# Layer 2 attention: reading in array quarters, rope rows of two heads in one tile, and a new order of the stages

## The reference, cut to what matters

```python
kv_c = kv @ W_kvc                                  # 64 latent numbers a key
q_c = q @ W_dq                                     # 96 numbers a query
q_nope = (q_c @ W_uq).reshape(b, lq, H, HD)        # H = 16 heads
q_rope = _rope((q_c @ W_qr).reshape(b, lq, H, R), lq)   # R = 64
k_nope = (kv_c @ W_uk).reshape(b, lk, H, HD)
v = (kv_c @ W_uv).reshape(b, lk, H, HD)
k_rope = _rope(kv_c @ W_kr, lk)
scores = (q_nope . k_nope + q_rope . k_rope) * scale
scores = where(good, scores, NEG)                  # a window of 8 keys
out = softmax(scores) @ v
x = x + out.reshape(b, lq, H * HD) @ W_o
```

## Time and profile before

| | |
|---|---|
| median of three runs | 2151.97 us |
| the profiled execution's own time | 2150.64 us |
| its span | 2148.5 us |
| busy share: TensorE, VectorE, ScalarE, GpSimd | 83%, 70%, 46%, 45% |
| Layer 2 attention, tile loop | 739.2 to 1217 us |
| mean granted clock of TensorE | 0.91 |

### The profile page before, as it was taken

The page is one execution under the profiler, slowest core; times in us unless marked ns, Lnnn a source line. Parts: engine busy times, 40 slices in busy tenths (PEclk is TensorE's granted clock), DMA queues, the critical chain, the costliest instruction groups (busy, mean ns, idle before and its releaser), DMA issues. The chain is left out here.

```text
span 2148.5 us, 42586 instructions
## 1 busy us (share of the span) xinstructions
PE 1773.9 (83%) x14235; PEld 1327.5 (62%) x14238; DVE 1510.6 (70%) x3427; ACT 980.3 (46%) x2343; POOL 956.9 (45%) x1091
## 2 busy tenths in 40 slices
PE   6989845399797599889898789889888986989993
PEld 5869712188575577777777568644444442557772
DVE  7875841276757789899898756689888983554446
ACT  3743131034323355455454334358787875523330
POOL 3420016543338366666666485314344433743330
PEclk9989955599899799999999899879999997999996
DMA  7831026530205000000000201037777753333337
GB/s 230 277 105 60 11 76 179 142 124 6 72 1 162 1 1 0 0 0 0 0 0 0 59 2 45 17 66 156 142 156 147 158 113 106 110 104 107 105 106 249
DMA packets 150747, 182.39 MB, mean 85 GB/s; under 512 B 40193, under 2 KB 132593, under 8 KB 146481
## 3 DMA queue, kind: packets, MB, share of 16 engines
q1 hardware_dynamic: 140769, 158.05, 28.4%
q0 software_dynamic: 9808, 22.23, 3.4%
HBM read 121.78 MB, written 56.79 MB: 83 GB/s over the span
## 5 line engine op out<-in xcount | busy, mean ns | idle before, releaser
L2874 DVE TENSOR_REDUCE mx<-banks 128x4 f32<-128x1024 f32 x256 | 309.5, 1221 | 47.9 <-PE banks L2746 44.1
L2846 ACT ACTIVATE e<-banks 128x512 f32<-128x512 f32 x512 | 280.5, 599 | 90.4 <-PE banks L2768 84.7
L1914 POOL TENSOR_TENSOR q_l<-q_l,rot_l 64x512 f32<-64x512 f32 x128 | 162.4, 1269 | 129.3 <-DVE rot_l L2112 129.3
L2783 PE MATMUL banks<-e,val 128*32 128x256 f32 x2048 | 169.5, 404 | 9.9 <-ACT nd L2841 8.3
L2768 PEld LDWEIGHTS banks<-q,k 64*128 64x128 f32 x1024 | 79.5, 192 | 127.3 <-ACT e L2846 99.6
L2768 PE MATMUL banks<-q,k 64*128 64x256 f32 x1024 | 133.2, 339 | 22.8 <-ACT e L2846 22.1
L2746 PE MATMUL banks<-k,q 62*128 62x256 f32 x1024 | 113.4, 302 | 19.8 <-DVE mx L2874 7.7
L1946 PE MATMUL banks<-qcT,wq_abs 96*128 96x128 f32 x1024 | 125.8, 282 | 0.0
L3061 POOL DMA_INDIRECT y<-y,y_row x71 | 69.0, 971 | 125.3 <-DVE y L3336 120.4
L1946 PEld LDWEIGHTS banks<-qcT,wq_abs 96*128 96x128 f32 x1024 | 120.0, 196 | 2.5
L1971 PE MATMUL banks<-wvo,rd_l 128*128 128x256 f32 x512 | 115.9, 379 | 0.0
(11 more groups left out here) (445 smaller groups left out, 4732.4 us busy)
## 6 DMA issues: line engine op xcount, KB each, us to landing
k<-k_parts SPq DMA_DIRECT2D x128, 128.0 KB, 5.3
q<-q_parts SPq DMA_DIRECT2D x64, 256.0 KB, 4.2
got<-rows SPq DMA_DIRECT2D x71, 129.0 KB, 2.2
k_parts<-k_parts_a SPq DMA_DIRECT2D x64, 128.0 KB, 3.3
moe_rows<-zero_a SPq DMA_DIRECT2D x16, 512.0 KB
w<-in_e0w SPq DMA_DIRECT2D x16, 512.0 KB
q_parts<-parts SPq DMA_DIRECT2D x64, 128.0 KB, 2.7
rec<-rec_rows SPq DMA_DIRECT2D x64, 128.0 KB, 2.5
```

The lines of the kernel that those rows point to most:

```text
L1914: nc.gpsimd.tensor_tensor(q[64:P, j, four(m), :], q[64:P, j, four(m), :], rot[64:P, j, four(m), :], ALU.add).then_inc(s["rope_added"], 1)
L2783: last = nc.tensor.matmul(readout[32 * g:32 * g + 32, side], val[:, a.n % 2, g, i, lt, :], e[:, slot(i, r), lt, :], start=(i == 0 and lt = ...
L2846: nc.scalar.activation(e[:, slot(i, r), :, :].rearrange("p k n -> p (k n)"), scoresT(i, r)[:, :], ACT.Exp).then_inc(s["exp_ready"], 1)
L2874: v.tensor_reduce(mx[:, a.n, :, 0, at:at + 2], c.banks[:, 2 * p:2 * p + 2, :].rearrange("p g (a n) -> p g a n", a=2), AX.X, ALU.max, negat ...
```

## The change

- **Layout of queries.** `wq` is rearranged: heads 0 to 7 of the 16 matmuls of `queries` now give the latent rows of a pair of heads each (`qa`, banks 0 and 1), heads 8 to 15 the rope rows of a pair of heads (`q`, banks 2 and 3). The count of matmuls and their shape stay. The table of cos and sin spans 128 partitions, and the sign moves into an instruction.
- **Rope.** Two groups instead of four; each is one product on 128 partitions and two on 64. GpSimd adds twice, on 128 partitions.
- **Copies.** `nope` has two copies of 128 partitions instead of four of 64. `key_copy` moves to ScalarE: four copies of 32 partitions into `key_r` and two of 64 into `key`.
- **Scores.** Split in two: `latent_scores`, twice 16 matmuls of 64 rows by 64 columns with 64 moving columns, in quarters of the array; then `rope_scores`, 16 matmuls of 128 rows by 64 columns with 128 moving columns, which add a pair of heads at a time.
- **Reading.** 16 matmuls of 64 rows by 64 columns with 128 moving columns instead of four of 128 by 128 with 256. ScalarE copies the result only when both halves are there.
- **Order on TensorE.** Features of t+3 and queries of t+2 come after the rope scores of t+1; latent scores of t+1 come between read and project of t. The wait for `x_done` of t now stands in the middle of `queries(t + 2)`.
- **Order on VectorE.** rope of t+1, maxima and sums of t+1, and only then back of t and stats of t.

```diff
             def softmax(t, j):
-                pool.wait_ge(s["rope_added"], quarters(t, 3))
+                pool.wait_ge(s["rope_added"], halves(t, 1))
...
-                for m in range(4):
-                    pool.wait_ge(s["rope_done"], quarters(t, m))
-                    nc.gpsimd.tensor_tensor(q[64:P, j, four(m), :], q[64:P, j, four(m), :], rot[64:P, j, four(m), :],
+                for m in range(2):
+                    pool.wait_ge(s["rope_done"], halves(t, m))
+                    nc.gpsimd.tensor_tensor(q[:, j, four(m), :], q[:, j, four(m), :], rot[:, j, four(m), :],
                                             ALU.add).then_inc(s["rope_added"], 1)
...
             def queries(t, j):
                 pe.wait_ge(s["qc_copied"], ready(t))
-                pe.wait_ge(s["x_done"], freed(t))
                 for h in range(H2):
+                    if h == HP:
+                        last.then_inc(s["qa_ready"], 1)
+                        pe.wait_ge(s["x_done"], freed(t))
                     last = nc.tensor.matmul(bank(j, h // 4)[:, (h % 4) * P:(h % 4 + 1) * P], wq[:, h, :],
                                             qcT[:, j, :], start=True, stop=True)
...
                     for b in range(2):
-                        last = nc.tensor.matmul(bank(j, n)[:, b * D:(b + 1) * D], kv2[:, j, b, :],
-                                                scT[:, j, four(n), 64 * b:64 * b + 64], start=True, stop=True)
+                        for col in range(2):
+                            for row in range(2):
+                                m = 4 * n + 2 * col
+                                out = bank(j, row)[side(col), n * D:(n + 1) * D].rearrange("p (i k q) -> p i k q", i=2, k=2)
+                                last = nc.tensor.matmul(out[:, :, b, :], kv2[side(row), j, b, side(col)],
+                                                        scT[side(row), j, m:m + 2, side(b)], start=True, stop=True)
...
+            def latent_scores(t, j, swap):
+                if swap == 0:
+                    pe.wait_ge(s["nope_copied"], ready(t))
+                    pe.wait_ge(s["key_ready"], ready(t))
+                else:
+                    pe.wait_ge(s["abs_done"], 4 * ready(t))
+                settle(pe, s["abs_passed"])
+                for n in range(4):
+                    for row in range(2):
+                        m = row ^ swap
+                        hp = 4 * m + n
+                        at = place(2 * hp + row) * S
+                        for b in range(2):
+                            last = nc.tensor.matmul(bank(j, m)[side(b), at:at + S], qa[side(row), j, hp, side(b)],
+                                                    key[side(row), j, side(b)], start=(swap == 0 and n == 0), stop=False,
+                                                    skip_group_check=True)
...
+            def rope_scores(t, j):
+                for m in range(2):
+                    pe.wait_ge(s["rope_added"], halves(t, m))
+                    for n in range(4):
+                        hp = 4 * m + n
+                        for b in range(2):
+                            pair = bank(j, m)[side(b), :].rearrange("p (c k n) -> p k c n", c=2, k=4)[:, place(2 * hp), :, :]
+                            last = nc.tensor.matmul(pair, q[:, j, hp, side(b)], key_r[:, j, b, :, :],
+                                                    start=False, stop=True, skip_group_check=True)
+                    last.then_inc(s["scores_ready"], 1)
...
-            def step(t, j, left=3):
-                if left > 1:
-                    queries(t + 1, 1 - j)
-                if left > 2:
-                    features(t + 2, j)
+            def step(t, j, left=4):
                 turn(t, j, 0)
                 if left > 2:
                     compress(t + 2, j)
                     pe.wait_ge(s["qc_copied"], ready(t + 2))
                 turn(t, j, 1)
                 read(t, j)
+                if left > 1:
+                    latent_scores(t + 1, 1 - j, 0)
+                    latent_scores(t + 1, 1 - j, 1)
                 project(t, j)
                 if left > 1:
-                    scores(t + 1, 1 - j)
+                    rope_scores(t + 1, 1 - j)
+                if left > 2:
+                    queries(t + 2, j)
+                if left > 3:
+                    features(t + 3, 1 - j)
...
             for t in range(NT):
                 j = t % 2
+                key_copy(t + 1, 1 - j)
                 exponent(t, j)
+                nope(t + 1, 1 - j)
                 features(t + 2)
                 turned(t, j, 0)
                 compress(t + 2)
                 turned(t, j, 1)
                 read(t, j)
-                nope(t + 1, 1 - j)
                 values(t + 1, 1 - j)
                 norm(t + 3)
...
-                for m in range(4):
...
+                for m in range(2):
+                    raw = bank(j, 2 + m)[:, :].rearrange("p (h n) -> p h n", h=4)
+                    tab = lambda ap, at: ap[at, :].unsqueeze(1).broadcast_to([at.stop - at.start, 4, P])
+                    v.tensor_tensor(q[:, j, four(m), :], raw, tab(c.cos, slice(0, P)), ALU.mult)
+                    v.tensor_tensor(rot[side(1), j, four(m), :], raw[side(0)], tab(c.sin, side(0)), ALU.mult)
+                    v.scalar_tensor_tensor(out=rot[side(0), j, four(m), :], in0=raw[side(1)], scalar=-1.0, in1=tab(c.sin, side(1)),
+                                           op0=ALU.mult, op1=ALU.mult).then_inc(s["rope_done"], 1)
...
             def step(t, j):
-                for n in range(2):
-                    maxima(t, j, n)
-                stats(t - 1)
-                for n in range(2):
-                    sums(t, j, n)
                 rope(t + 1, 1 - j)
+                softened(t + 1, 1 - j)
                 back(t, j)
+                stats(t)
```

More of the change, by code:

```diff
@@ L1973, in project @@
                 last.then_inc(s["out_ready"], 1)
[L1975 to L1986, removed]
@@ L2008, in _ @@
             queries(0, 0)
-            scores(0, 0)
-            with pe.Fori(0, NT // 2 - 1) as i:
+            latent_scores(0, 0, 0)
+            latent_scores(0, 0, 1)
+            rope_scores(0, 0)
+            queries(1, 1)
+            features(2, 0)
+            with pe.Fori(0, NT // 2 - 2) as i:
                 step(2 * i, 0)
                 step(2 * i + 1, 1)
+            step(NT - 4, 0)
+            step(NT - 3, 1, 3)
             step(NT - 2, 0, 2)
@@ L2051, in read, with key_copy @@
                 act.wait_ge(s["out_ready"], freed(t))
-                for n in range(2):
-                    act.wait_ge(s["read_ready"], halves(t, n))
-                    act.copy(rd[:, j, four(n), :].rearrange("p h (b q) -> p b h q", b=2),
-                             bank(j, n)[:, :].rearrange("p (b h q) -> p b h q", b=2, h=4)).then_inc(s["read_copied"], 1)
+                act.wait_ge(s["read_ready"], halves(t, 1))
+                for row in range(2):
+                    pairs = rd[:, j, :, :].rearrange("p (n r i) q -> p r n (i q)", n=2, r=2)
+                    act.copy(pairs[:, row, :, :],
+                             bank(j, row)[:, :].rearrange("p (n k) -> p n k", n=2)).then_inc(s["read_copied"], 1)
+            def key_copy(t, j):
+                if t >= NT:
+                    return
+                act.wait_ge(s["scores_ready"], halves(t - LANES, 1))
+                tile_keys = c.keysT[:, t * P:t * P + P]
+                for n in range(2):
+                    for x in range(2):
+                        at = 64 * x + 32 * n
+                        act.copy(key_r[at:at + 32, j, :, n, :],
+                                 tile_keys[64 + 32 * x:96 + 32 * x, :].rearrange("p (b n) -> p b n", b=2))
+                    last = act.copy(key[side(n), j, :], tile_keys[0:64, :])
+                last.then_inc(s["key_ready"], 1)
             def nope(t, j):
@@ L2070, in values @@
                 for b in range(2):
-                    for r in range(2):
-                        last = act.copy(kv2[64 * r:64 * r + 64, j, b, 64 * r:64 * r + 64],
-                                        at_tile(c.kvc, t)[64 * b:64 * b + 64, :])
+                    for row in range(2):
+                        last = act.copy(kv2[side(row), j, b, :].rearrange("p (c n) -> p c n", c=2),
+                                        at_tile(c.kvc, t)[side(b), :].unsqueeze(1).broadcast_to([64, 2, 64]))
                 last.then_inc(s["kv_ready"], 1)
-            act.wait_ge(s["l_zero"], 1)
             norm(0)
             norm(1)
+            act.wait_ge(s["key_zero"], 1)
+            key_copy(0, 0)
             features(0)
@@ L2136, in stats @@
                 v.bn_stats(at_tile(c.bn, t), at_tile(c.x, t))
-            def step(t, j):
-                for n in range(2):
-                    maxima(t, j, n)
-                stats(t - 1)
-                for n in range(2):
-                    sums(t, j, n)
-                rope(t + 1, 1 - j)
-                back(t, j)
```

76 lines of the change are left out of this document (34 added, 42 removed).

## The result

The changed kernel takes **2319.6 us** (median of four runs, 2316.8 to 2323.4) against 2151.7 us before (median of four): a ratio of 1.079, 95% interval 1.076 to 1.081. It is 168 us slower. The prediction was 2265 us, 2215 to 2310: the right side and, as will be seen, the right place, but 55 us short and 10 us outside its own range.

The account below looks back on a forecast made before the run. It took VectorE to bound the old tile, 14.9 us, and the moved wait plus half clock to make 18.8: 30 x (18.8 - 14.9) = 117, less 4, so 2150.6 + 113 + 1.3 = 2265 us, range 2215 to 2310.

Parts of the forecast that it names:

- The moved wait: In the middle of queries, TensorE waits for back of VectorE, now behind the sums: a pause of 3.3 us a tile.
- The cycle at full clock: One tile, from the mask of half 0 to the next, without half clock: 17.7 us, +2.8.
- The clock: TensorE falls to half clock after the pause in queries: 1.1 us a tile more, giving 18.8 us.
- this very pause: The empty window at 1204 us in the old trace, where the last tile has no queries to cover its softmax.
- the end of 2.6 us for the clock: Longer low stretches on TensorE: 2.6 us a tile instead of 1.1, 2310 us; the longer-stretches rival had chance 0.08.
- the 0.5 us either way on the cycle: Allowance on the time of one tile, used for the forecast range.
- the lower end: Rival that TensorE's clock stays up despite the pause: 30 x 2.8 - 4 = 80, 2232 us, chance 0.20.
- Work costs: Per tile: VectorE -4.3 us for rope, GpSimd additions 2.1 to 2.6, ScalarE key copy 1.5 to 3.6, TensorE equal.
- Quarters of the array run together: In read and latent scores on TensorE, four matmuls run at once: 0.95 us each; the pairs rival had chance 0.10.
- the 9.8 us of VectorE: VectorE's work per tile after the change: about 9.8 us, no longer the bound by its work.
- The rival on the other side: No pause in queries, x_done comes before TensorE reaches their middle: about 14.9 us a tile, 2120 to 2150 us, chance 0.07.

Follow-up runs that it names:

- before_back_late: The kernel before, with VectorE's back and stats of t-1 moved behind the sums of t, shapes untouched: 2378.8 us, 1.097 of the kernel before.
- back_first: The changed kernel, with VectorE's back and stats of t moved ahead of the maxima and sums of t+1: 2183.2 us, 1.007 of the kernel before.
- fill_half: The changed kernel, with TensorE making the first four matmuls of queries twice: 1.061 of the kernel before.
- fill_once: The changed kernel, with TensorE making the first eight matmuls of queries twice: 1.053 of the kernel before.
- tuned_order: The changed kernel, with its orders on TensorE, VectorE and ScalarE rewritten: 2124.8 us, 0.981 of the kernel before.
- project_last: The changed kernel, with TensorE's project of t moved behind the rope scores of t+1: 2149.9 us, 0.991 of the kernel before.
- fill_twice: The changed kernel, with TensorE making the first eight matmuls of queries three times: 1.050 of the kernel before.
- quarters_apart: project_last, with read and latent scores loops turned so one row half of the array comes before the other: 1.001 of the kernel before.

## Why the prediction was right in its place and wrong in its size

**The moved wait: right.** The cycle was written as mask to x_done 6.0 us; measured 964.48 - 958.59 = 5.9. The pause was forecast at 3.3 us and is 3.33. before_back_late and back_first show that where back stands causes it.

**The cycle at full clock: 0.45 us short.** Forecast 17.7 us, measured 18.15 (the tiles of fill_half and fill_once without half clock). Most of it is between the latent scores and project: 1.2 us forecast, 974.07 - 972.54 = 1.5 measured, since the second 32 records start 0.9 us behind the first (972.54 to 973.44 in the trace) and project another 0.63 behind them, about when they end; the prediction had 0.95 + 0.25 for all of it. Project to the next group took 3.65 (977.72 - 974.07), not 3.55. That is 30 x 0.45 = 14 us of the error.

**The clock: the step that failed.** The mechanism was right, the pause brings the half clock on; the size of its term was wrong. The prediction took one stretch of 3.4 us at half clock, less what falls into waits, as 1.1 us a tile. Measured are 6.8 us at half clock in each of 30 tiles, 5.4 of them over work, and a cost of 2.3 us: 30 x 1.2 = 36 us, most of the 55. The better row was in hand. The end of the old stage has the same pause, and its clock was 0.50 for 5.2 us behind it; it was called "this very pause" and then used as the upper end instead of as the value. Of the three pauses of the earlier trace rows it is also the nearest in kind: turn, read and project follow it, as here. Read like the windows of the changed kernel above, even have its 6.8 us: a mean of 0.77 over 3.6 us is 1.7 us at half clock in the pause, and 5.2 follow. The view behind the earlier trace rows also has a fourth pause, of 2.6 us at 683.9, with 0.50 for the 3.4 us behind it; so three of the four pauses, and not two of three, spoke for the half clock:

```profile
683.90:686.50 2.60, 0.04 (x2) 0.00 (x1) 2.60 (x8) 1.07 (x3) 2.58 (x5) 1.00 0.93 287
687.30:690.70 3.40, 3.40 (x10) 2.69 (x9) 3.33 (x9) 0.06 (x1) 3.40 (x5) 0.50 0.60 170
```

What decides between 3.4 and 6.8 us behind a pause stays open beyond what the three fill runs show.

**The range.** With the end of 2.6 us for the clock the prediction's own sum was 2310, and the 0.5 us either way on the cycle was not added on top of it, as it was at the lower end (2232 - 15 = 2217). Both went the same way: 2265 + 36 + 14 = 2315; the last 5 us to the measured 2320 are not traced. Two errors of one sign on a number multiplied by 30 tiles need the room.

**Work costs: right.** Rope products on 128 partitions take 0.69 us as on 64; six a tile. The addition on 128 partitions takes 1.27, the upper of the two rows taken as bounds. Key copies cost 1.8 us of ScalarE a tile, and no wait of TensorE from 740 to 1380 us is put down to them. Quarters of the array run together. TensorE's work came out equal, as forecast: before it was busy 179.06 of 200 us (800 to 1000 us), with 14.9 us a tile 13.3 us; in tuned_order, where it hardly waits, 197.00 of 200, with 13.4 us a tile 13.2. Only the 9.8 us of VectorE don't follow from the rows: 44.47 of 50 us are 13.3 us a tile, less 4.3 is 9.0. Measured are 9.4 (183.16 us of the 400 in the two windows of the changed kernel), and nothing hung on it.

**The rival on the other side** had the right threshold: x_done had to come before TensorE reached the middle of queries. With 14.9 us a tile it was close to back_first, 15.4, which waits for the softmax in turn 0 as that rival said. Its 2120 to 2150 us are 2 to 32 us under the kernel before; project_last, where the pause is gone by another way, lies in them with 15. The 41 us of tuned_order lie beyond every rival: the new shapes are worth more once the order is rewritten around them.

## What to carry to other kernels

An engine's written order is part of the critical path: before moving an instruction behind another, ask which engine waits for its semaphore and what that engine has in hand to do until then. Count the work that covers a latency (here all of queries, 3.8 us, then half of them) rather than the share of busy time, which fell on every engine while the kernel slowed down. When a pause of TensorE of some microseconds recurs in each round, price the clock from the row with the same pause and the same work behind it, and try filling the pause with useless matmuls: if that makes the kernel faster, the clock is what costs.

## What the runs showed of the hardware that was not expected

- A pause of 3.3 us in each tile cost 6.8 us at 1.2 GHz, every time, 30 tiles in a row, twice the 3.4 us that a stretch lasts in fill_once; they came at the tile's own rhythm of 20.5 us. Pauses of 1.5 us, with eight more matmuls ahead of them (fill_once), cost one stretch of 3.4 us in about every second tile, and with no pause (fill_twice) the clock stays at 1.00. The page TensorE: Matmul & The Clock Gate of the Trainium skill, HAM oscillation, says that a wait for data repeated in each round of a loop (some 3 to 5 us in its case) makes every round start cold. The changed kernel, whose pause is 3.3 us, agrees in all 30 tiles. The 1.5 us of fill_once are shorter than the waits of that case, and still brought the half clock in about half of the tiles. TensorE with 16 useless matmuls a tile is 61 us faster, by distance from the kernel before, than without them (107 against 168).
- Matmuls in quarters of the array started together four at a time (0.05 us from the first to the fourth), and in quarters_apart those of the read did so even where all four matmuls of one row half are written ahead of the four of the other: the last record of the first half was the 14th of 16 to start.
